# Attention scores from two exact 12-bit parts in rounded single precision, two heads in the two halves of TensorE's rows

## The reference

```python
qk = jnp.einsum('bthd,bshd->bhts', qh, kh)
qk = jnp.where(causal, qk, -jnp.inf)
attn = jax.nn.softmax(qk, axis=-1)
qkv = jnp.einsum('bsdh,bhts->bthd', vh, attn)
```

## Time and profile before

| what | value |
|---|---|
| median of 3 runs | 857.16 us (854.01 to 859.2) |
| the profiled execution's own time | 856.38 us |
| its span in the profile | 854.6 us |
| mean granted clock of TensorE | 0.987 of full |
| busy: TensorE / its weight loads | 780.8 / 361.9 us |
| busy: VectorE / ScalarE / GpSimd | 554.1 / 581.7 / 184.0 us |
| ScalarE's exps, L856 | 576, 530.9 us |
| VectorE's maxima, L1284 | 640, 373.5 us |

### The profile page before, as it was taken

How to read it: one execution, slowest core, us unless ns; L and a number is a source line. 1 busy time by engine, 2 the same in 40 slices (tenths; PEclk the granted TensorE clock), 3 DMA queues, 4 the chain that set the end, 5 groups by cost and what they waited for, 6 DMA issues and landing times.

```text
span 854.6 us, 27793 instructions
## 1 busy us (share of the span) xinstructions
PE 780.8 (91%) x11935; PEld 361.9 (42%) x11935; DVE 554.1 (65%) x1207; ACT 581.7 (68%) x683; POOL 184.0 (22%) x356
## 2 busy tenths in 40 slices
PE   1478999999999999999999989999999899999994
PEld 1243334443444444444444444443444443444443
DVE  6877334777776767766677777667677777321216
ACT  1257787776767787788777767666666577666572
POOL 4453112101121102111211021100210721223222
PEclk9999999998999999999999999999999999999997
DMA  3112332005130002000300030000400102200003
GB/s 107 58 60 78 125 101 79 3 2 105 42 113 3 3 3 73 2 3 2 114 3 3 2 113 2 2 3 2 150 3 2 46 7 75 61 13 17 17 19 99
DMA packets 29375, 36.64 MB, mean 43 GB/s; under 512 B 6190, under 2 KB 24014, under 8 KB 28998
## 3 DMA queue, kind: packets, MB, share of 16 engines
q1 hardware_dynamic: 27862, 32.03, 12.8%
q0 software_dynamic: 1248, 2.57, 0.9%
q10 hardware_dynamic: 144, 0.27, 0.1%
HBM read 24.25 MB, written 10.24 MB: 40 GB/s over the span
## 4 chain that ended last, share of the span: by engine, by line
PE 76%; DVE 13%; ACT 5%; issue 4%; DMA 0%; POOL 0%; POOLq 0%; ACTq 0%; DVEq 0%
PE PS L973 24%; PE PS L953 23%; PE PS L919 13%; DVE MP L1284 5%; ACT PR L856 4%; PE PS L998 3%; PE PS L982 2%; PE PS L1015 2%; PE PS L923 2%; PE PS L1038 1%; DVE OT L1305 1%; PE PS L997 1%; PE PS L891 1%; DVE KA L1214 1%; PE PS L1006 1%
## 5 line engine op out<-in xcount | busy, mean ns | idle before, releaser
L856 ACT ACTIVATE PR<-PS 128x1024 f32<-128x1024 f32 (+1 forms) x576 | 530.9, 975 | 159.3 <-PE PS L953 157.3
L1284 DVE TENSOR_REDUCE MP<-PS 128x1 f32<-128x512 f32 (+3 forms) x640 | 373.5, 608 | 124.9 <-PE PS L919 69.3
L953 PE MATMUL PS<-QA,KA 74*32 74x512 bf16 (+3 forms) x5120 | 333.6, 351 | 8.1 <-ACT PR L856 7.4
L973 PE MATMUL PS<-PR,VA 128*32 128x512 f32 (+3 forms) x2560 | 287.8, 533 | 3.8 <-DVE OT L1305 2.6
L919 PE MATMUL PS<-KA,QA 72*32 72x512 bf16 (+3 forms) x2560 | 229.5, 352 | 13.3 <-DVE MP L1284 10.9
L676 POOL TENSOR_SCALAR_AFFINE_SELECT PR<-PR 128x256 f32<-128x256 f32 x256 | 102.2, 416 | 481.8 <-ACT PR L856 476.0
L953 PEld LDWEIGHTS PS<-QA,KA 74*32 74x32 bf16 x5120 | 118.2, 97 | 156.2 <-ACT PR L856 68.2
L919 PEld LDWEIGHTS PS<-KA,QA 72*32 72x32 bf16 x2560 | 69.2, 95 | 119.2 <-DVE MP L1284 79.7
L973 PEld LDWEIGHTS PS<-PR,VA 128*32 128x32 f32 x2560 | 73.4, 110 | 51.4 <-issue 13.4
L923 PE MATMUL PS<-CM,IDB 128*32 128x128 bf16 x1024 | 57.7, 220 | 0.0
L1425 DVE SCALAR_TENSOR_TENSOR FC<-FC,PS 128x256 f32<-128x256 f32 x23 | 9.7, 421 | 61.8 <-ACT FC L839 61.8
(11 more groups left out here) (177 smaller groups left out, 408.4 us busy)
## 6 DMA issues: line engine op xcount, KB each, us to landing
QA<-q_parts SPq DMA_DIRECT2D x96, 96.0 KB
KA<-k_parts SPq DMA_DIRECT2D x48, 96.0 KB
QA<-in_W SPq DMA_DIRECT2D x1, 2048.0 KB, 7.5
q_parts<-QA SPq DMA_DIRECT2D x4, 384.0 KB, 2.6
q_parts<-KA SPq DMA_DIRECT2D x4, 384.0 KB, 2.5
expert_tokens<-ZERO SPq DMA_DIRECT2D x1, 1483.5 KB, 12.7
QA<-expert_tokens SPq DMA_DIRECT2D x1, 1483.5 KB, 7.3
KA<-k_shared SPq DMA_DIRECT2D x48, 24.0 KB
```

What stands on the lines that cost most here:

```text
L856: act.activation(PR[:, (2 * n + p) % RING, :, 0:w], PS[:, 2 * p:2 * p + 2, 0:w], ACT.Exp)\
L953: last = pe.matmul(PS[r:r + STRIP, hh, start:start + CH - q0], KA[0:ROWS, b, kb // BPC, 0 if ffn else hh, key:key + STRIP], QA[0:ROWS, b, ...
L973: last = pe.matmul(PS[32 * hh:32 * hh + 32, 6, q0:CH], VA[:, slot % 2, kb, hh, :], PR[:, (2 * n + hh // 2) % RING, hh % 2, start:start + C ...
L1284: dve.reduce_max(MP[:, BPC * (HG * (qb // BPC) + hh) + qb % BPC, kc:kc + 1], PS[:, 4 + u % 2, 0:item_width(item)], AX).then_inc(s_mr, 1)
```

## The change

Each of q and k becomes two parts: the top 12 bits of the significand (a mask of the low 12 bits, `TOP_BITS`), and what is left. The four products of parts take 4 x 8 = 32 rows, with three more for the shift, 35 (`ROWS`); the maxima use 33. The stacks are of the type `float32r`, single precision that TensorE rounds. They have rows 0 to 34 for one head and 64 to 98 for another, so that two heads (`par`) lie in the two halves of the array's rows. Each half has all 128 keys, or queries, as its columns, with no strips, and writes a bank of its own. A maxima unit is now two heads in banks 4 and 5 (320 units), with one reduce over both; the mask is four matmuls of 64 rows. The units of a step come in two parts, and the values move between the scores of the two halves of a step. The ring of probabilities has 7 pairs. ScalarE copies q and k out of PSUM whole, and VectorE splits them with two operations. Memory layouts, loads, stores and the rows of the shift follow.

```diff
-STACK = PARTS * PARTS * HD
-ROWS = STACK + 2
-STRIP = 32
+
+TOP_BITS = -4096
+STACK = 4 * HD
+MAXROWS = STACK + 1
+ROWS = STACK + 3
+HALFROWS = P // 2
...
-RING = 8
+RING = 7
...
+            for half, share in enumerate((0.3, 0.7)):
+                own += share * (width(SEQ[n][1]) + 400)
+                if n in HOLD:
+                    continue
+                while u < UNITS and (n == end - 1 and half or done * total < own * work):
+                    out[n][half].append((a, u // 2, u % 2))
+                    done += item_width(u // 2) + 64
+                    u += 1
...
+                for par in range(2):
+                    out.append((("unit", unit_number(u), par), 4 + par, "M"))
...
+        Q2 = sb("Q2", [P, NC, 2, CH], F32R)
+        K2 = sb("K2", [P, NC, 2, CH], F32R)
...
-                for j in range(PARTS):
-                    sp.dma_start(QA[r * j:r * (j + 1), b, c, :, :].rearrange("p h s -> p (h s)"),
-                                 QP[c][j, g].rearrange("d h s -> d (h s)").unsqueeze(1)
-                                 .broadcast_to([HD, PARTS, HG * CH])).then_inc(s_st[b][c], 16)
-                for j in range(PARTS):
+                for par in range(2):
+                    rows = half(par, STACK)
+                    sp.dma_start(QA[b][rows, c, :, :].bitcast(F32).rearrange("p a s -> p (a s)"),
+                                 QP[c][g, par].rearrange("j d a s -> (j d) (a s)").unsqueeze(1)
+                                 .broadcast_to([2 * HD, 2, 2 * CH])).then_inc(s_st[b][c], 16)
                     if g < NKV:
-                        sp.dma_start(KA[r * j:r * (j + 1), b, c, 0, :], KPF[c][:, g].rearrange("i d s -> d i s"))\
-                          .then_inc(s_st[b][c], 16)
+                        sp.dma_start(KA[b][rows, c, 0, :].bitcast(F32),
+                                     KPF[c][g].rearrange("d i s -> (d i) s").unsqueeze(0)
+                                     .broadcast_to([2, 2 * HD, CH])).then_inc(s_st[b][c], 16)
                     else:
-                        sp.dma_start(KA[r * j:r * (j + 1), b, c, :, :].rearrange("p h s -> p (h s)"),
-                                     KPA[c][:, g - NA].rearrange("i d h s -> d i (h s)")).then_inc(s_st[b][c], 16)
+                        sp.dma_start(KA[b][rows, c, :, :].bitcast(F32).rearrange("p a s -> p (a s)"),
+                                     KPA[c][g - NA, par].rearrange("d i a s -> (d i) (a s)").unsqueeze(0)
+                                     .broadcast_to([2, 2 * HD, 2 * CH])).then_inc(s_st[b][c], 16)
...
+            sp.wait_ge(s_one, 32 * 2)
             ones(2)
+            sp.wait_ge(s_cs, 32 * 2)
+            constant_shift(2)
...
+                q = qb % BPC * P
+                for par in range(2):
+                    free(("unit", u, par))
+                    rows = half(par, MAXROWS)
+                    last = pe.matmul(PS[:, 4 + par, 0:w], QA[b][rows, c, pair, q:q + P], KA[b][rows, kc, pair, 0:w],
+                                     start=True, stop=not diag)
                 if diag:
-                    for r in range(0, P, STRIP):
-                        last = pe.matmul(bank[r:r + STRIP, w - P:w], IDB[:, r:r + STRIP], CM[:, :],
-                                         start=False, stop=True)
+                    for i in range(2):
+                        for par in range(2):
+                            rows = half(par, HALFROWS)
+                            last = pe.matmul(PS[:, 4 + par, w - P:w], HALVES[rows, i, :], HALVES[rows, 2 + i, :],
+                                             start=False, stop=i == 1)
                 last.then_inc(s_mm, 1)
...
-                for k in range(2):
-                    hh = 2 * p + k
-                    for kb, q0, start in parts:
-                        for r in range(0, P, STRIP):
-                            key = kb % BPC * P + r
-                            last = pe.matmul(PS[r:r + STRIP, hh, start:start + CH - q0],
-                                             KA[0:ROWS, b, kb // BPC, 0 if ffn else hh, key:key + STRIP],
-                                             QA[0:ROWS, b, c, hh, q0:CH], start=True, stop=True)
+                        pe.wait_ge(s_sh[b][c], 64 * (before + 1))
+                for kb, q0, start in parts:
+                    key = kb % BPC * P
+                    for par in range(2):
+                        rows = half(par, ROWS)
+                        last = pe.matmul(PS[:, 2 * p + par, start:start + CH - q0],
+                                         KA[b][rows, kb // BPC, 0 if ffn else p, key:key + P],
+                                         QA[b][rows, c, p, q0:CH], start=True, stop=True)
...
-                for p in range(2):
-                    if n < N:
-                        scores(n, p)
-                    for unit in parts[p]:
-                        max_unit(unit)
+                if n < N:
+                    scores(n, 0)
+                for unit in parts[0]:
+                    max_unit(unit)
                 if 0 <= n - LAG < N:
                     values(n - LAG)
+                if n < N:
+                    scores(n, 1)
                 if ended(n - LAG - 1) is not None:
                     turn(ended(n - LAG - 1))
-                for unit in parts[2]:
+                for unit in parts[1]:
...
-            def remainder(n):
+            def split(n):
                 key, dst, factor = source(n)
-                w = dst.shape[2]
-                if n >= 2:
-                    dve.wait_ge(s_lo, n - 1)
-                dve.wait_ge(s_hi, n + 1)
-                dve.scalar_tensor_tensor(RES[:, n % 2, 0:w], PS[:, BANK[key], 0:w], factor, dst[:, 0, :],
-                                         ALU.mult, ALU.subtract).then_inc(s_res, 1)
-                dve.wait_ge(s_res, n + 1)
-                dve.sem_inc(s_rd, 1)
-
-            def split(n):
-                remainder(n)
-                key, dst, factor = source(n)
-                rest = RES[:, n % 2, 0:dst.shape[2]]
-                dve.tensor_copy(dst[:, 1, :], rest).then_inc(s_mid, 1)
+                read(dve, key)
+                dve.tensor_scalar(dst[:, 0, :].bitcast(I32), dst[:, 1, :].bitcast(I32), TOP_BITS, None, ALU.bitwise_and)\
+                   .then_inc(s_mid, 1)
                 dve.wait_ge(s_mid, n + 1)
-                dve.tensor_tensor(dst[:, 2, :], rest, dst[:, 1, :], ALU.subtract).then_inc(s_lo, 1)
+                dve.tensor_tensor(dst[:, 1, :], dst[:, 1, :], dst[:, 0, :], ALU.subtract).then_inc(s_lo, 1)
...
+                col_ = MP[:, m * (qb // BPC):m * (qb // BPC + 1), kc].rearrange("p (a b t) -> p a b t", a=2, b=2)
+                dve.reduce_max(col_[:, :, pair, qb % BPC], PS[:, 4:6, 0:item_width(item)], AX).then_inc(s_mr, 1)
```

More of the change, by code:

```diff
@@ L118, in spread_maxima @@
 def spread_maxima():
-    out = [[] for _ in range(N)]
+    out = [([], []) for _ in range(N)]
     for a, (first, end) in enumerate(MAX_SPAN):
         total = sum(width(SEQ[n][1]) + 400 for n in range(first, end))
-        work = HG * sum(item_width(i) + 64 for i in range(len(ITEMS)))
+        work = 2 * sum(item_width(i) + 64 for i in range(len(ITEMS)))
         u = done = own = 0
         for n in range(first, end):
[L126 to L132, removed]
+            for half, share in enumerate((0.3, 0.7)):
[6 more added lines that the diff above has]
+                    u += 1
     return out
@@ L200, in bank_uses @@
         parts = maxima_at(n)
[L201 to L206, removed]
+        for half in range(2):
+            if half and ended(n - LAG - 1) is not None:
+                out.append((("turn", ended(n - LAG - 1)), 7, "D"))
+            for u in parts[half]:
+                for par in range(2):
+                    out.append((("unit", unit_number(u), par), 4 + par, "M"))
         for name, k in works(n):
@@ L247, with build @@
 NL = 912
-K_ID, K_TRI, K_CM, K_EARLIER, K_BEFORE, K_RANK, K_TOK, K_SPARE, K_TILE, K_J, K_OWN = 0, 128, 256, 384, 520, 584, 592, 608, 631, 654, 670
-NK = 678
-def build(nc, x, front, late, const, W1, W2, b1, b2, out):
+K_ID, K_TRI, K_EARLIER, K_BEFORE, K_RANK, K_TOK, K_SPARE, K_TILE, K_J, K_OWN = 0, 128, 256, 392, 456, 464, 480, 503, 526, 542
+NK = 550
+NHALF = 4 * P
+def build(nc, x, front, late, const, halves, W1, W2, b1, b2, out):
     with ExitStack() as ctx:
@@ L319, in build @@
         HBG, KNS, HGAMMA, HBETA = (HALF[:, i:i + 1] for i in range(4))
[L321 to L338, removed]
+        KS2 = FC[:, 0, :].rearrange("p (a i n) -> p a i n", a=2, i=2)
         XTF = AOA[:, :, :].rearrange("p t n -> p (t n)")
@@ L1047, in work @@
                     pe.wait_ge(s_nm, k + 1)
-                    pe.matmul(bank[0:2 * HG * BPC, 0:P], NMR[:, :, :].rearrange("p a n -> p (a n)"), IDB[:, :],
-                              start=True, stop=True).then_inc(s_fl, 1)
+                    pe.transpose(bank[0:HG * BPC, 0:P], NM[:, :], ID).then_inc(s_fl, 1)
                 if name == "O":
@@ L1476, in _ @@
```

(8 more changed lines are left out.)

249 lines of the change are left out of this document (130 added, 119 removed).

## The result

The changed kernel takes 1219.6 us in the median (1209.4 to 1226.3, 4 runs) against 858.2 us, a ratio of 1.421, 95% interval 1.410 to 1.433. I had forecast 845. The profiled execution's span is 1217.3 us.

The account below looks back on a forecast made before the run. TensorE was taken to bound the kernel: long stage 342 streaming + 76 other + 54 changes + 104 waits = 576 us against 579 (-3); elsewhere -5, -3, -2; together -13, forecast 845 us, range 795 to 905.

Parts of the forecast that it names:

- five cases: Whole kernel: gain nearly eaten, 0.46; changes or waits cheaper, 0.21; (c), 0.18; (d), 0.11; (e), 0.04.
- the long stage: Steps 34 to 256, the stage with the maxima: forecast 576 us against 579.
- Streaming: TensorE, long stage: scores 90, values 180, maxima 58, masks 14, together 342 us, with one pass and halves side by side.
- (d): Scores and maxima: the two halves do not run side by side, about 1000 us; chance 0.11.
- (e): Scores and maxima: rounded single precision takes four passes, about 1300 us; chance 0.04.
- Changes of shape: TensorE between scores and values: two changes a step at 0.12 us each, 54 us in the long stage; bounds 0 and 89.
- weight loads: TensorE's loads of 128 columns for the two halves: taken at nothing, hidden under the matmuls in flight.
- my bound of 58: Long stage: weight loads passing in series delay blocks behind a change of shape by up to 0.13 us, up to 58 us.
- case (c): Slower by weight loads: the halves' loads pass in series, 0.13 us a block, 903 us at full price; chance 0.18.
- Waits for the reduce: Long stage: the next maxima unit waits for VectorE's whole two-bank reduce, 104 us on TensorE; bounds 50 and 130.
- The 13.3 us that I took off: Long stage: the old kernel's TensorE waits for VectorE's reduce, subtracted from 89 us of other work to leave 76.
- SyncE's constant rows: Third buffer's constant rows on SyncE's queue: claimed issued steps ahead of their readers, at no cost.

Follow-up runs that it names:

- Filled rows: The changed kernel with 29 spare rows of each half zeroed and multiplied too (64 rows a half), maxima from step 44: 994.0 us, against 876.5 before on the same chip.
- the bf16 run: The changed kernel with scores and maxima reading only the upper 16 bits of each part as bf16: 950.9 us, against 864.1 before on the same chip.
- the run over 56 rows: The kernel before the change, with scores and maxima over the first 56 of 74 rows: 950.2 us, against 873.4 unedited on the same chip.
- the filled kernels: Versions of the changed kernel multiplying 64 rows a half, spare rows filled, maxima from step 44 or 46, some with further edits: 991.5 to 1157.2 us.

## Why the prediction was wrong

**The failed step is one that wasn't taken.** "At 2.4 GHz 512 columns are 0.213 us" was carried from before into every streaming term of the sum, and none of my five cases had a clock of its own. The trace before granted 0.99 in the long stage, and I took that for a property of the kernel, not a result of what it multiplies. The stage forecast at 576 us took 916. Filled rows with ten steps fewer took 651; those ten steps without units are an estimated 16 us (1.6 us each at 0.43 + 0.85 + 0.3), so some 250 of the 340 us of the miss are the clock. Shown: with all else equal, more rows in each matmul lift the clock (35 to 64 in the change, 35 to 56 in the old kernel). Shown as well: a shorter reduce and bf16 operands each lift it from 0.64 to 0.86 without more rows, and with either the stage gets about as short (627 and 657 us) as with filled rows. Not shown is how the three combine. The number of rows alone doesn't tell the level: 56 rows in use kept 0.97 in the old kernel, 70 in the bf16 run 0.84. The Trainium skill, TensorE: Matmul & The Clock Gate, Part 1, makes the clock a matter of how busy the engine has been. The traces don't agree that the busy share tells it: TensorE was busy 92% of the long stage (839.78 of 916.10 us) at 0.56, and 83% of the filled kernel's (539.51 of 651.30 us) at 0.95.

**Streaming: right.** One pass, side by side, 0.21 us for two heads at the upper level. Cases (d) and (e) are out. The range of 795 to 905 us did not hold the 1219.6 us, since it was drawn at the upper level only.

**Changes of shape and weight loads: 0.24 us a step forecast, more measured.** At full clock the values are followed after 1.00 us, 0.15 late. The scores behind them delay the unit by 0.13 (443.87 to 444.21, 0.34 for 0.213), and the last scores delay the values by 0.15 (444.45 to 444.81, 0.36 for 0.213): 0.42 us a step. The 0.12 us of the earlier trace rows was about right for the change alone, as the run over 56 rows shows. The weight loads that I took at nothing are most of the rest: 0.18 us a step over 223 steps is 40 us, and the filled kernels give 32 to 47 of my bound of 58. That was case (c), with a chance of 0.18. The Trainium skill's drain at a change of tiling mode (TensorEngine Tiling (Array Packing), Key Properties) is borne out by 0.11 us a change.

**Waits for the reduce: right in size.** 104 us forecast; at full clock 102 us of matmul idle time end on the reduce. Part of this may be luck: the filled kernels begin the maxima ten or twelve steps later, and no run checks how the 104 us were put together. In the change itself, at the lower clock, it is 70 us. The reduce of 1024 takes 1.23 us as reckoned. That VectorE and ScalarE don't bind was right too. The 13.3 us that I took off as the old waits for the reduce are 10.9 in the earlier trace rows, which changes nothing.

**The pause: missed.** I wrote that SyncE's constant rows "are issued steps ahead of their readers and cost nothing". They stand behind the loads of the third buffer, the ones take 11.5 us to land, and the first unit reads them: 18.3 us.

**Put together at the upper level**, the stage would be 651 + 16 less what its clock of 0.95 costs, an estimated 640 us against 579 before and 576 forecast. So the change would have been slower even without the fall of the clock, by some 60 us in the stage and 18 for the pause. The weight loads are 32 to 47 of the 64 us that the stage's forecast lacks; the rest is open. Neither sign nor size was mine.

## What to carry to other kernels

Before halving the rows or the time of a matmul, ask what keeps TensorE's clock up: here 35 rows in place of 64 cost 272 us in a stage in which the waits for the reduce cost about 100. A busy TensorE is no sign of a full clock. If a change thins the matmuls, forecast both clock levels and give the lower one a chance. Rows of zeros, multiplied along, brought the clock back, but they have to be put there cheaply.

## What the runs showed of the hardware

The granted clock rose with the rows named by the matmuls even when the added rows held zeros: 0.646 to 0.696 with 35 rows and a late start of the maxima, 0.921 to 0.946 with 64 rows of which 29 were zeros. Over 35 rows TensorE ran for 100 us without a pause at a clock of 0.50. Matmuls over 56 rows pay 0.11 us at each change to or from matmuls over 128 rows; matmuls over 72 rows don't. A transfer that writes three partitions in pieces of 512 bytes took 11.5 us, with the loads issued ahead of it on the same queue.
